# State sums, gate and output turn of a Mamba scan: from channels in rows to tokens in rows

## The chip, the core and the metric

The kernel runs on one core of a Trainium2 chip. The metric is the device time of one execution in microseconds, the median over runs. The five engines of a core (TensorE or PE, VectorE or DVE, ScalarE or ACT, GpSimd or POOL, SyncE or SP) each work through their own queue in order and meet only at semaphores.

## The reference, cut to what matters

One layer of Mamba with a residual and two norms, then a mixture of experts, for x of 8 sequences x 512 tokens x 256 channels. The part that the change touches:

```python
x_ssm, x_gate = split(x @ in_proj_w.T + in_proj_b)
x_conv = silu(conv4(x_ssm) + conv_b)
B, C = split(x_conv @ bc_w.T + bc_b)
dt = softplus(x_conv @ dt_w.T + dt_b)
# for each of 512 steps, 16 states n for each of 256 channels d
h = h * exp(dt[:, None] * A) + dt[:, None] * B[None, :] * x[:, None]
y = sum_n(h * C) + x * D
out = (y * silu(x_gate)) @ out_w.T + out_b + x      # then layer norms
```

After it, a router (8 experts, the 4 best of each token), experts of 512 inner channels with a clipped gate, the weighted sum and a last layer norm.

## The kernel before

Two big stages share one program. Stage 1 does the Mamba layer, the router and the scatter of rows to the experts' queues in DRAM; stage 2 runs the experts over tiles of 512 queued rows; a short last part does the final norm.

**Stage 1.** A sequence is held with channels in the 128 partitions, two halves of 256 channels, and its 512 tokens along the row. Work goes in rounds, one for each sequence, and every engine's program walks the same 16 slots of a round (`for r in rounds(...)`, `for t in range(SLOTS)`), one slot for each of the 16 states. The order inside a slot is written by hand for each engine. Rounds 3 to 6 are a hardware loop. A round works on several sequences at once: sequence s+1 is projected, convolved and prepared (flag `r.a`), s is scanned (`r.b`), s-1 is gated, projected out and normed (`r.c`), s-2 is routed (`r.d`).

In slot t DVE forms the scan's input (`weigh_inputs`, L1032) and scans 128 x 1024 (`scan`, L1041). ACT makes the decays two slots ahead (`decays`, L822), through a ring of four tiles. POOL multiplies the state by C one slot behind (`read_state`, L1175). PE adds the result two slots behind (`sum_states`, L632 to L642): for each half one f32 matmul with the identity as weights, 512 columns, that accumulates into the PSUM bank `p_y[h]`. The first of a sequence is preceded by x times D, a matmul with a diagonal matrix (L638). An f32 matmul shows as two MATMUL instructions in the trace, a transpose as one.

In slot 2 of the next round DVE's `gate` (L1049) multiplies `p_y` by silu of the gate, waits for the sixteenth sum, writes `y` (channels in partitions) and sets `s_y`. Right behind it DVE reads the router's result (`rank_experts`, L1065). In slot 5 DVE's `take_counts` (L1098) waits for PE's `count` (L683 to L687). PE's order from slot 2 on is: `project` 0 and 1, the sum of slot 0 with its x times D, `project_out` 0 and 1 (`y` as weights, so that its result has tokens in partitions), the sum of slot 1, `count`, `convolve`. ACT takes the output in slot 4 (`take_out`, L844), then come the first norm (`variance`, `apply_norm`), POOL's `scale` and DVE's `residual` in slot 9.

Small products of PE go through two PSUM banks, `p_bank`, taken in turn by a list of names (`Round.blocks`); each name waits until the one two places earlier has been read. In slot 8 PE makes `dt0`, `dt1` and `bc`, in slots 10 and 11 the two halves of the gate (`project(r, 2)` and `(r, 3)`), which ACT stores with their bias (`store_in`, L763) and later turns to silu (`silu_gate`).

Of the kernel before, what the change touches and what calls it, by code (L numbers as in the profile page):

```python
# [9 lines left out]
BF16 = mybir.dt.bfloat16  # L10
# [6 lines left out]
P = 128  # L17
# [36 lines left out]
class Round:  # L54
# [13 lines left out]

    def blocks(self):
        d, a, c = self.d, self.a, self.c  # L70
        return (["tr0", "tr1", "rt"] * d + ["in0", "in1"] * a + ["o0", "o1"] * c + ["cnt"] * d + ["cv0", "cv1"] * a
                + ["dt0", "dt1", "bc", "in2", "in3"] * a)

    def block(self, name):
# [90 lines left out]
def build(nc, ctx, ins, out):  # L165
    def sem(name):
        return ctx.enter_context(nc.semaphore(name))

    def sb(name, *shape, dt=F32, at=ctx):
        return at.enter_context(nc.sbuf_tensor(name, [P, *shape], dt))  # L170
# [91 lines left out]
    b_parts = sb("b_parts", D, dt=BF16, at=one)  # L262
    x = sb("x", TT, D, at=one)
    y = sb("y", HALVES, LEN, at=one)
    z = sb("z", TT, D, at=one)
    row_sum = sb("row_sum", 2, TT, at=one)
    var = sb("var", 2, TT, at=one)
# [29 lines left out]
    s_offset, s_t = sem("s_offset"), sem("s_t")  # L297
    s_route, s_rexp, s_chosen, s_index = (sem(n) for n in ("s_route", "s_rexp", "s_chosen", "s_index"))
    s_table = sem("s_table")
    s_scrap = sem("s_scrap")  # L300
    s_left = sem("s_left")
    s_scat = [sem(f"s_scat{i}") for i in range(2)]
# [265 lines left out]
    def pe_stage1(pe):  # L568
        pe.wait_ge(s_first, FIRST_SETUP)

        def order_rate():

            pe.wait_ge(s_const, SETUP)
            for h in range(HALVES):
                mm = pe.transpose(p_y[h][0:STATE, 0:P], raw_rate[:, STATE * h:STATE * (h + 1)], ident[:, :])
            mm.then_inc(s_order, 1)
# [27 lines left out]
        def project(r, m):  # L604
# [3 lines left out]
                pe.wait_ge(s_xt, 16 * (r.s.at(1).n + 1))  # L608
            product(bank[:, :], columns(IN + m * P, P), lambda k: xt[:, k, :]).then_inc(done, 1)

        def convolve(r, h, some):

            if r.like == Round.FIRST:
                pe.wait_ge(s_set_dve, 2)
            if 0 in some:
                bank, _ = block(r, f"cv{h}")
                src, n = r.block(f"in{h}")
                pe.wait_ge(bank_read[src], n)
            b, _ = r.block(f"cv{h}")
            for j in some:  # L620
                mm = pe.matmul(p_bank[b][:, :], taps[:, TAPS * h + j, :], xpad[:, h, j:j + LEN],
                               start=(j == 0), stop=(j == TAPS - 1))
            if TAPS - 1 in some:
                mm.then_inc(bank_full[b], 1)
# [7 lines left out]
        def sum_states(s, t):  # L632

            n = SLOTS * s.n + t
            if t == 0:
                after(pe, s_y, s.n)
                for h in range(HALVES):
                    pe.matmul(p_y[h][:, :], skip_w[:, h, :], xc[s.p][:, h, :], start=True, stop=False)  # L638
            pe.wait_ge(s_read, n + 1)
            for h in range(HALVES):  # L640
                mm = pe.matmul(p_y[h][:, :], ident[:, :], read[:, t % 4, h, :], start=False, stop=(t == SLOTS - 1))  # L641
            mm.then_inc(s_added, 1)  # L642

        def project_out(r, b):

            bank, done = block(r, f"o{b}")
            s = r.s.at(-1)
            if b == 0:
                pe.wait_ge(s_y, s.n + 1)
            for i in range(2):  # L650
                to = bank[:, i * D:(i + 1) * D]
                at = (2 * b + i) * P
                product(to, lambda k: y[:, k, at:at + P], columns(OUT, D), stop=False)
                pe.matmul(to, ones[0:3, :], b_parts[0:3, :], start=False, stop=False)
                if b == 0 and i == 0:
                    pe.wait_ge(s_offset, s.n + 1)
                mm = pe.matmul(to, ident[:, :], x[:, 2 * b + i, :], start=False, stop=True)
            mm.then_inc(done, 1)
# [20 lines left out]
        def count(r):  # L679
# [9 lines left out]
                               skip_group_check=True)  # L689
            mm.then_inc(done, 1)  # L690

        for r in rounds(pe):
            for t in range(SLOTS):
                if t < 2 and r.c:
                    sum_states(r.s.at(-1), SLOTS - 2 + t)
                if r.last and t == 0:
                    transpose_tile(pe, Seq(0, 0))
                    up_projection(pe, Seq(0, 0), 0)
                if r.d and t == 0:
                    transpose_rows(r, 0)  # L700
                    transpose_rows(r, 1)
                if r.d and t == 1:
                    route(r)
                if r.a and t == 2:
                    project(r, 0)
                    project(r, 1)
                if r.c and t == 3:
                    project_out(r, 0)
                    project_out(r, 1)
                if r.last and t == 4:  # L710
                    up_projection(pe, Seq(0, 0), 1)
                if r.d and t == 4:
                    count(r)
                if r.a and t == 4:
                    convolve(r, 0, range(TAPS))
                if r.a and t in (5, 6):
                    half = TAPS // 2 * (t - 5)
                    convolve(r, 1, range(half, half + TAPS // 2))
                if r.like == Round.FIRST and t == 5:
                    order_rate()  # L720
                if r.a and t == 8:
                    for i in range(HALVES):
                        from_xc(r, f"dt{i}", DT_ + i * P, P)
                    from_xc(r, "bc", BC, 2 * STATE)
                if r.like == Round.FIRST and t == 9:
                    place_rate()
                if r.a and t in (10, 11):
                    project(r, t - 8)
                if t >= 2 and r.b:
                    if t == 2 and r.like == 0:  # L730
                        pe.wait_ge(s_set_dve, SET_DVE)
                    sum_states(r.s, t - 2)


    def act_stage1(act):
# [20 lines left out]
        def store_in(r, m):  # L756

            s = r.s.at(1)
            bank, done = full(act, r, f"in{m}")
            if m == 2:  # L760
                after(act, s_y, s.n - 1)
            to = xpad[:, m, TAPS - 1:TAPS - 1 + LEN] if m < 2 else sg[s.p][:, m - 2, :]
            act.activation(to, bank[:, :], ACT.Identity, bias=b_in[:, m:m + 1]).then_inc(done, 1)  # L763

        def store_conv(r, h):
            s = r.s.at(1)
# [65 lines left out]
        def start_total(r):  # L832
# [3 lines left out]
            act.dma_start(total_rows[bass.ds(s.n, 1), :, :, :].rearrange("s p t d -> (s p) t d"),  # L836
                          rows[s.p][:, :, 0:D]).then_inc(s_total[s.p], 16)

        def take_out(r, b):

            bank, done = full(act, r, f"o{b}")
            for i in range(2):
                t = 2 * b + i
                last = act.activation(z[:, t, :], bank[:, i * D:(i + 1) * D], ACT.Copy, accum_out=row_sum[:, 0, t:t + 1])  # L844
            last.then_inc(done, 1)
# [32 lines left out]
        for r in rounds(act):  # L878
            for t in range(SLOTS):

                if r.d and t == 3:
                    router_exp(r)
                if r.a and t == 7:
# [68 lines left out]
    def dve_setup(dve):  # L952

        dve.memset(table[:, :], 0.0).then_inc(s_set_dve, 1)
        dve.wait_ge(s_first, FIRST_SETUP)
        for i in range(HALVES * TAPS):
            dve.tensor_scalar(taps[:, i, :], ident[:, :], tap[:, i // TAPS, i % TAPS:i % TAPS + 1], None, ALU.mult)
        for h in range(2):
            last = dve.memset(xpad[:, h, 0:TAPS - 1], 0.0)
        last.then_inc(s_set_dve, 1)  # L960
        steps = Steps(dve, s_raw, 0, 10)
        steps.then(dve.tensor_tensor(b_bc[:, :], b_bc[:, :], b_or_c[:, :], ALU.mult))
        dve.tensor_reduce(b_bc2[:, :], b_bc[:, :], AX.X, ALU.add).then_inc(s_set_dve, 1)

        dve.wait_ge(s_const, SETUP)
        steps.then(dve.tensor_tensor(b_rest[:, :], b_out[:, :], ln_b[:, :], ALU.subtract))
        steps.then(dve.memset(b_parts[:, :], 0.0))
        for i in range(3):
            steps.then(dve.tensor_copy(b_part[:, :], b_rest[:, :]))
            if i < 2:  # L970
                steps.then(dve.tensor_tensor(b_rest[:, :], b_rest[:, :], b_part[:, :], ALU.subtract))
            steps.then(dve.scalar_tensor_tensor(b_parts[:, :], b_part[:, :], ident[:, i:i + 1], b_parts[:, :],
                                                ALU.mult, ALU.add))

    def dve_setup_rest(dve):
        dve.memset(neg_half[:, :], -0.5)
# [21 lines left out]
    def dve_stage1(dve):  # L998
# [45 lines left out]
        def gate(r):  # L1044
            s = r.s.at(-1)
            dve.wait_ge(s_added, SLOTS * (s.n + 1))
            dve.wait_ge(s_silu, 2 * s.n + 2)
            for h in range(HALVES):
                last = dve.tensor_tensor(y[:, h, :], p_y[h][:, :], sg[s.p][:, h, :], ALU.mult)  # L1049
            last.then_inc(s_y, 1)  # L1050

        def residual(r):
# [634 lines left out]
```

## Time and profile before

| | us |
|---|---|
| median of 3 runs | 1368.25 (1363.77 to 1369.27) |
| profiled execution, its own time | 1371.27 |
| its span, first to last instruction | 1369.4 |
| PE busy, share of the span | 1168.3, 85% |
| DVE busy | 1061.2, 77% |
| ACT busy | 899.0, 66% |
| POOL busy | 792.0, 58% |
| start of the first and of the last `drive` (L1023) | 36.5 and 538.0 |

The page gives the busy time of each engine, the span in 40 slices, the chain that ended last and the costliest groups of instructions. PE counts as busy while a matmul is in its pipeline. The granted clock of TensorE is given for any stretch as a share of full speed: 1.00 is 2.4 GHz, 0.50 is 1.2 GHz; between them a stretch holds both.

### The profile page before, as it was taken

Reading aid. Unit: us, or ns where it says so; the run is one execution under the profiler, and the core shown is the slowest. Engines: PE = TensorE matmul, PEld = TensorE weight load, DVE = VectorE, ACT = ScalarE, POOL = GpSimd, SP = SyncE. Lnnn points to the kernel's source line nnn. Section 1 sums busy time; section 2 is a strip of 40 time slices with the busy share of each in tenths; the row PEclk is TensorE's granted clock in tenths of the full one; section 3 lists DMA queues with packets and bytes.
Section 4 is the critical chain, followed back from the end, with each engine's and each line's share of the span. In section 5 each row is a group of like instructions: output and inputs, shape, how many; then the busy total and the mean of one; then the engine's idle time right before and its main releaser. Section 6 shows DMA issues by size and latency. Waiting matters only on the chain. (4 is left out here: it accounts for less than half of the span.)

```text
span 1369.4 us, 18063 instructions
## 1 busy us (share of the span) xinstructions
PE 1168.3 (85%) x5138; PEld 802.5 (59%) x5138; DVE 1061.2 (77%) x1558; ACT 899.0 (66%) x1551; POOL 792.0 (58%) x566
## 2 busy tenths in 40 slices
PE   7879697988969797765799999999999999999940
PEld 3324252434334343324588888888888888888840
DVE  2999899999989999994777777777777777777744
ACT  4775849485856768425467777767767776767734
POOL 0457568888878888897643444444444444444342
PEclk9899999999999999887899999999999999999985
DMA  2543434545443545336676655566565655565537
GB/s 97 206 155 123 171 107 172 172 149 180 146 167 149 205 150 170 136 104 241 233 216 161 161 144 136 149 158 160 158 160 159 160 139 138 147 163 159 159 38 246
DMA packets 69258, 217.18 MB, mean 159 GB/s; under 512 B 7520, under 2 KB 43232, under 8 KB 56288
## 3 DMA queue, kind: packets, MB, share of 16 engines
q1 hardware_dynamic: 29664, 167.42, 34.0%
q0 software_dynamic: 26880, 36.72, 15.7%
q10 hardware_dynamic: 12672, 12.58, 2.8%
q8 instruction: 14, 0.23, 0.1%
q14 instruction: 28, 0.23, 0.1%
HBM read 165.54 MB, written 51.15 MB: 158 GB/s over the span
## 5 line engine op out<-in xcount | busy, mean ns | idle before, releaser
L641 PE MATMUL p_y<-read,small 128*128 128x512 f32 x512 | 260.4, 644 | 84.2 <-POOL read L1175 84.2
L1041 DVE TENSOR_TENSOR_SCAN state<-decay,p_bu 128x1024 f32<-128x1024 f32 x128 | 292.5, 2285 | 19.3 <-ACT decay L822 10.2
L1497 POOL DMA_INDIRECT total<-o_v,tok x144 | 266.0, 1847 | 45.4 <-issue 45.3
L641 PEld LDWEIGHTS p_y<-read,small 128*128 128x128 f32 x512 | 100.8, 205 | 226.9 <-POOL read L1175 123.3
L1495 POOL TENSOR_TENSOR scrap<-neg_half 128x1 f32<-128x1 f32 x36 | 13.0, 362 | 319.8 <-ACT o_v L1404 317.3
L822 ACT ACTIVATE decay<-dt,scan_rate 128x511 f32<-128x511 f32 x256 | 165.2, 713 | 20.6 <-DVE state L1041 20.2
L1175 POOL TENSOR_TENSOR read<-state,bc 128x1024 f32<-128x1024 f32 x64 | 150.2, 2353 | 34.5 <-DVE p_bu L1032 17.6
L505 ACT ACTIVATE gate_v<-p_g,bias 128x512 f32<-128x512 f32 x144 | 98.5, 684 | 103.0 <-PE p_up L495 96.8
L1217 POOL DMA_INDIRECT queues<-rows,index x128 | 134.4, 1050 | 31.7 <-issue 28.9
L1391 ACT ACTIVATE ah<-a_v 128x512 fp32r<-128x512 f32 x144 | 91.2, 633 | 93.0 <-DVE a_v L519 89.3
L1175 POOL TENSOR_TENSOR read<-state,first_wh 128x1024 f32<-128x1024 f32 x32 | 75.4, 2357 | 65.3 <-DVE p_bu L1032 51.7
L513 DVE TENSOR_SCALAR up_v<-up_v 128x512 f32<-128x512 f32 x144 | 61.5, 427 | 66.6 <-ACT up_v L508 55.7
L1442 DVE TENSOR_TENSOR al<-a_v,ah 128x512 fp32r<-128x512 f32 x144 | 98.8, 686 | 12.4 <-ACT ah L1391 12.4
L519 DVE SCALAR_TENSOR_TENSOR a_v<-gate_v,up_v 128x512 f32<-128x512 f32 x144 | 99.7, 692 | 4.9
L508 ACT ACTIVATE up_v<-p_up,bias 128x512 f32<-128x512 f32 x144 | 98.2, 682 | 0.0
L1175 POOL TENSOR_TENSOR read<-state,first_wl 128x1024 f32<-128x1024 f32 x32 | 75.2, 2352 | 31.2 <-DVE p_bu L1032 21.5
L1364 PE MATMUL p_o<-first_wh,ah 128*128 128x256 f32 x288 | 83.2, 289 | 3.9 <-DVE al L1442 3.9
L1032 DVE TENSOR_TENSOR p_bu<-p_u,bc 128x1024 f32<-128x1024 f32 x64 | 78.9, 1233 | 7.0 <-DVE state L1041 0.5
L1364 PE MATMUL p_o<-wh,ah 128*128 128x256 f32 x288 | 81.9, 284 | 1.6 <-DVE al L1442 1.6
L1364 PE MATMUL p_o<-first_wl,ah 128*128 128x256 f32 x288 | 81.4, 283 | 0.0
L1364 PE MATMUL p_o<-first_wh,al 128*128 128x256 f32 x288 | 81.3, 282 | 0.0
L1364 PE MATMUL p_o<-wh,al 128*128 128x256 f32 x288 | 80.4, 279 | 0.0
(222 smaller groups left out, 3014.7 us busy)
## 6 DMA issues: line engine op xcount, KB each, us to landing
bc<-bc_rows SPq DMA_DIRECT2D x32, 1024.0 KB, 4.9
first_raw<-in_w_experts SPq DMA_DIRECT2D x19, 1668.0 KB
raw_w<-in_w_experts SPq DMA_DIRECT2D x18, 1668.0 KB
first_wh<-bc_rows SPq DMA_DIRECT2D x16, 1024.0 KB
first_wl<-bc_rows SPq DMA_DIRECT2D x16, 1024.0 KB
first_rows<-queues SPq DMA_DIRECT2D x19, 544.0 KB
xq<-queues SPq DMA_DIRECT2D x18, 544.0 KB
queues<-pad SPq DMA_DIRECT2D x9, 544.0 KB
```

The source lines that it names most:

```text
L505: act.activation(gate_v[i % 2][:, :], p_g[i % 2][:, :], ACT.Silu, bias=bias[t.p][:, 0, i:i + 1], scale=ALPHA)
L508: act.activation(up_v[i % 2][:, :], p_up[i % 2][:, :], ACT.Identity, bias=bias[t.p][:, 1, i:i + 1])\
L519: dve.scalar_tensor_tensor(a_v[i % 2][:, :], gate_v[i % 2][:, :], TOP, up_v[i % 2][:, :], ALU.min, ALU.mult)\
L641: mm = pe.matmul(p_y[h][:, :], ident[:, :], read[:, t % 4, h, :], start=False, stop=(t == SLOTS - 1))
L822: act.activation(decay[t % AHEAD][:, h, 1:LEN], dt[s.p][:, h, 1:LEN], ACT.Exp, scale=rate[:, h, t:t + 1])\
L1041: dve.tensor_tensor_scan(flat(state[t % 4][:, :, :]), flat(decay[t % AHEAD][:, :, :]), p_bu[:, :], 0.0, ALU.mult, ALU.add).then_inc(s_stat ...
L1175: pool.tensor_tensor(read[:, t % 4, :, :], state[t % 4][:, :, :], of_state(t, 1), ALU.mult).then_inc(s_read, 1)
L1217: pool.indirect_dma_start(queues, bass.IndirectOffsetOnAxis(ap=index[s.p][:, i:i + 1], axis=0), rows[s.p][:, i // TOPK, :], None).then_inc ...
L1364: mm = pe.matmul(to, v[:, i, a * P:(a + 1) * P], w[t.p][:, c:c + D], start=(i == 0 and a % 2 == 0 and m == 0), stop=(i == CH - 1 and m == ...
L1391: act.activation(ah[:, i, :], a_v[i % 2][:, :], ACT.Copy).then_inc(s_ah, 1)
L1442: dve.tensor_tensor(al[:, i, :], a_v[i % 2][:, :], ah[:, i, :].bitcast(F32), ALU.subtract).then_inc(s_al, 1)
L1497: pool.indirect_dma_start(total, bass.IndirectOffsetOnAxis(ap=tok[t.p][:, a:a + 1], axis=0), o_v[t.p][:, a, :], None, compute_op=ALU.add). ...
```

## The change

Four parts. (1) `sum_states`: the product of state and C is now the weights, and the identity the moving operand, in 128 x 128 blocks with the transpose flag, eight for each slot, accumulating in PSUM; `p_y` then holds tokens in partitions. x times D becomes eight f32 matmuls of 128 columns for two of 512. (2) The gate is projected with tokens in partitions; since its bias then lies along the row, it is added by a bf16 matmul of three rows of `gate_parts`, the bias split in three bf16 parts, which are made at the start. (3) `gate` writes `y_rows`; PE turns it back with eight transposes through two more turns of the small banks (`turn_rows`), ACT copies them to `y` (`take_turned`), and `project_out` waits for both copies. (4) ACT stores the gate with Copy, without a bias.

```diff
-        return (... ["in0", "in1"] * a + ["o0", "o1"] * c + ["cnt"] * d + ...
+        return (... ["in0", "in1"] * a + ["yt0", "yt1", "o0", "o1"] * c + ["cnt"] * d + ...
@@ pe_stage1
+        def spread_gate_bias():
+            for h in range(HALVES):
+                mm = pe.matmul(p_bu[:, h * P:(h + 1) * P], b_in[:, HALVES + h:HALVES + h + 1].broadcast_to([P, P]),
+                               ident[:, :], start=(h == 0), stop=True, skip_group_check=True)
+            mm.then_inc(s_gate_bias, 1)
+        def project_gate(r, b):
+            bank, done = block(r, f"in{HALVES + b}")
+            if r.like == Round.FIRST and b == 0:
+                pe.wait_ge(s_set_dve, 4)
+            for i in range(2):
+                to, at = bank[:, i * D:(i + 1) * D], (2 * b + i) * P
+                product(to, lambda k: xt[:, k, at:at + P], lambda k: w[:, k, IN + D:IN + 2 * D], stop=False)
+                mm = pe.matmul(to, ones[0:3, :], gate_parts[0:3, :], start=False, stop=True)
+            mm.then_inc(done, 1)
@@ sum_states
+            def of_rows(h, b):
+                return p_y[b // 2][:, b % 2 * D + h * P:b % 2 * D + (h + 1) * P]
                 for h in range(HALVES):
-                    pe.matmul(p_y[h][:, :], skip_w[:, h, :], xc[s.p][:, h, :], start=True, stop=False)
+                    for b in range(TT):
+                        pe.matmul(of_rows(h, b), xc[s.p][:, h, b * P:(b + 1) * P], skip_w[:, h, :],
+                                  start=(h == 0 and b % 2 == 0), stop=False, skip_group_check=True)
             for h in range(HALVES):
-                mm = pe.matmul(p_y[h][:, :], ident[:, :], read[:, t % 4, h, :], start=False, stop=(t == SLOTS - 1))
+                for b in range(TT):
+                    mm = pe.matmul(of_rows(h, b), read[:, t % 4, h, b * P:(b + 1) * P], ident[:, :], is_transpose=True,
+                                   start=False, stop=(t == SLOTS - 1), skip_group_check=True)
+        def turn_rows(r, h):
+            bank, done = block(r, f"yt{h}")
+            if h == 0:
+                pe.wait_ge(s_y, r.s.at(-1).n + 1)
+            for b in range(TT):
+                mm = pe.transpose(bank[:, b * P:(b + 1) * P], y_rows[:, b, h * P:(h + 1) * P], ident[:, :])
+            mm.then_inc(done, 1)
@@ project_out
-            if b == 0:
-                pe.wait_ge(s_y, s.n + 1)
+            for h in range(HALVES):
+                src, n = r.block(f"yt{h}")
+                pe.wait_ge(bank_read[src], n)
@@ the loop of PE
+        spread_gate_bias()
                 if r.c and t == 3:
+                    turn_rows(r, 0)
+                    turn_rows(r, 1)
                     project_out(r, 0)
                 if r.a and t in (10, 11):
-                    project(r, t - 8)
+                    project_gate(r, t - 10)
@@ act_stage1, store_in for m of 2 and 3
+                last = act.activation(sg[s.p][:, m - 2, :], bank[:, :], ACT.Copy)
+        def take_turned(r, h):
+            bank, done = full(act, r, f"yt{h}")
+            act.activation(y[:, h, :], bank[:, :], ACT.Copy).then_inc(done, 1)
@@ the loop of ACT, ahead of all else in slot 3
+                if r.c and t == 3:
+                    take_turned(r, 0)
+                    take_turned(r, 1)
@@ dve_setup; in_parts is the loop that made b_parts before
+        dve.wait_ge(s_gate_bias, 1)
+        steps.then(dve.tensor_copy(b_rest[:, :], p_bu[:, 0:D]))
+        in_parts(gate_parts)
@@ gate
-                last = dve.tensor_tensor(y[:, h, :], p_y[h][:, :], sg[s.p][:, h, :], ALU.mult)
+                last = dve.tensor_tensor(flat(y_rows[:, 2 * h:2 * h + 2, :]), p_y[h][:, :], sg[s.p][:, h, :], ALU.mult)
```

## Rows read from the trace of the kernel before

The views cut runs of one kind of instruction together: x8 at the end of a row means eight instructions, and the time is that of all of them.

**Rows 1.** The page's first part, busy us and share of each engine.
```profile
PE 1168.3 (85%) x5138; PEld 802.5 (59%) x5138; DVE 1061.2 (77%) x1558; ACT 899.0 (66%) x1551; POOL 792.0 (58%) x566
```

**Rows 2.** Waits of DVE from 100 to 700 us: total us, times, longest.
```profile
DVE state L1041 <- ACT decay L822: 10.2, 13, 1.5
...
DVE place L1098 <- PE p_bank L687: 5.2, 3, 3.4
```

**Rows 3.** Timeline of PE, one round: start us, us, what, [idle before <-releaser].
```profile
397.94 1.98 PE L641 MATMUL p_y<-read,small 128*128 128x512 f32 x4 [3.08 <-POOL read L1175]
...
404.68 1.98 PE L598 MATMUL p_bank<-first_raw,w 128*128 128x512 f32 x4 [1.26 <-DVE lg L1065]
406.50 1.88 PE L638 MATMUL p_y<-xc,skip_w 128*128 128x512 f32 x4
408.22 1.88 PE L641 MATMUL p_y<-read,small 128*128 128x512 f32 x4
409.94 1.03 PE L598 MATMUL p_bank<-w,y 128*128 128x256 f32 x4
...
418.49 0.24 PE L687 MATMUL p_bank<-chosen,ones 128*128 128x32 bf16 x4
```

**Rows 4.** Timeline of DVE in the same round.
```profile
404.45 0.18 DVE L1065 TENSOR_TENSOR lg<-p_bank,small 128x32 f32<-128x32 f32 x1
...
417.59 1.23 DVE L1032 TENSOR_TENSOR p_bu<-p_u,bc 128x1024 f32<-128x1024 f32 x1
418.77 0.19 DVE L1098 TENSOR_TENSOR place<-p_bank,base 128x32 f32<-128x32 f32 x1
```

**Rows 5.** Timeline of PE, next round: eight transposes and what follows.
```profile
470.94 1.04 PE L665 MATMUL p_bank<-small,rows 128*128 128x128 f32 x8
471.81 1.88 PE L641 MATMUL p_y<-read,small 128*128 128x512 f32 x4
```

**Rows 6.** Timeline of PE, last rounds: transposes, then matmuls on their copies.
```profile
646.56 1.07 PE L665 MATMUL p_bank<-small,rows 128*128 128x128 f32 x8
648.46 1.92 PE L675 MATMUL p_bank<-small,x1t 128*128 128x8 f32 x16 [0.83 <-ACT x1t L871]
```

**Rows 7.** Timeline of PE where the clock was low.
```profile
462.00 5.13 PE L641 MATMUL p_y<-read,small 128*128 128x512 f32 x8 [5.46 <-POOL read L1175]
...
551.34 3.78 PE L638 MATMUL p_y<-xc,skip_w 128*128 128x512 f32 x4 [2.40 <-DVE y L1049]
554.91 2.96 PE L641 MATMUL p_y<-read,small 128*128 128x512 f32 x4
```

**Rows 8.** Stretches: busy us (x) of PE, PEld, DVE, ACT, POOL; PEclk; DMA.
```profile
393.00:396.00 3.00, 1.85 (x11) 1.09 (x9) 1.73 (x2) 1.47 (x3) 0.46 (x1) 1.00 0.01 4
...
462.00:465.00 3.00, 3.00 (x4) 1.44 (x5) 2.86 (x3) 2.99 (x5) 2.83 (x2) 0.51 0.97 288
```

**Rows 9.** Timeline of PE, then of ACT, at the dt projection of that round.
```profile
433.64 3.70 PE L598 MATMUL p_bank<-xc,w 128*128 128x512 f32 x8 [1.06 <-ACT xc L776]
...
438.50 0.68 ACT L790 ACTIVATE first_raw<-p_bank,small 128x512 f32<-128x512 f32 x1
...
440.68 0.68 ACT L813 ACTIVATE bc_out<-p_bank,b_bc 32x512 f32<-32x512 f32 x1 [0.93 <-PE p_bank L598]
```

**Rows 10.** Timeline of PE, then of DVE, at the start.
```profile
6.05 6.12 PE L598 MATMUL p_bank<-first_raw,w 128*128 128x512 f32 x8 [6.05 <-DMA small<-in_small]
...
9.52 0.43 DVE L966 TENSOR_TENSOR b_rest<-set_up,small 128x256 f32<-128x256 f32 x1 [1.56 <-DMA set_up<-in_set_up]
...
13.19 0.48 DVE L972 SCALAR_TENSOR_TENSOR b_parts<-b_part,small,b_parts 128x256 bf16<-128x256 bf16 x1
...
31.63 1.23 DVE L1005 SCALAR_TENSOR_TENSOR rest<-rest,expo 128x1024 f32<-128x1024 f32 x1 [14.72 <-ACT rest L801]
```

**Rows 11.** Timeline of PE, then of DVE, after the last scan.
```profile
620.04 1.10 PE L598 MATMUL p_bank<-w,y 128*128 128x256 f32 x4 [1.22 <-DVE y L1049]
...
627.24 0.19 DVE L1098 TENSOR_TENSOR place<-p_bank,base 128x32 f32<-128x32 f32 x1 [3.42 <-PE p_bank L687]
```

More of the change, by code:

```diff
@@ L70, in blocks @@
         d, a, c = self.d, self.a, self.c
-        return (["tr0", "tr1", "rt"] * d + ["in0", "in1"] * a + ["o0", "o1"] * c + ["cnt"] * d + ["cv0", "cv1"] * a
+        return (["tr0", "tr1", "rt"] * d + ["in0", "in1"] * a + ["yt0", "yt1", "o0", "o1"] * c + ["cnt"] * d + ["cv0", "cv1"] * a
                 + ["dt0", "dt1", "bc", "in2", "in3"] * a)
@@ L264, in build @@
     y = sb("y", HALVES, LEN, at=one)
+    y_rows = sb("y_rows", TT, D, at=one)
+    gate_parts = sb("gate_parts", D, dt=BF16, at=one)
     z = sb("z", TT, D, at=one)
@@ L299, in build @@
     s_table = sem("s_table")
+    s_gate_bias, s_y_rows = sem("s_gate_bias"), sem("s_y_rows")
     s_scrap = sem("s_scrap")
@@ L761, in store_in @@
                 after(act, s_y, s.n - 1)
-            to = xpad[:, m, TAPS - 1:TAPS - 1 + LEN] if m < 2 else sg[s.p][:, m - 2, :]
-            act.activation(to, bank[:, :], ACT.Identity, bias=b_in[:, m:m + 1]).then_inc(done, 1)
+            if m < 2:
+                last = act.activation(xpad[:, m, TAPS - 1:TAPS - 1 + LEN], bank[:, :], ACT.Identity, bias=b_in[:, m:m + 1])
+            else:
+                last = act.activation(sg[s.p][:, m - 2, :], bank[:, :], ACT.Copy)
+            last.then_inc(done, 1)
         def store_conv(r, h):
@@ L963, in dve_setup, with in_parts @@
         dve.tensor_reduce(b_bc2[:, :], b_bc[:, :], AX.X, ALU.add).then_inc(s_set_dve, 1)
+        def in_parts(to):
+            steps.then(dve.memset(to[:, :], 0.0))
+            for i in range(3):
+                steps.then(dve.tensor_copy(b_part[:, :], b_rest[:, :]))
+                if i < 2:
+                    steps.then(dve.tensor_tensor(b_rest[:, :], b_rest[:, :], b_part[:, :], ALU.subtract))
+                steps.then(dve.scalar_tensor_tensor(to[:, :], b_part[:, :], ident[:, i:i + 1], to[:, :], ALU.mult, ALU.add))
+        dve.wait_ge(s_gate_bias, 1)
+        steps.then(dve.tensor_copy(b_rest[:, :], p_bu[:, 0:D]))
+        in_parts(gate_parts)
         dve.wait_ge(s_const, SETUP)
         steps.then(dve.tensor_tensor(b_rest[:, :], b_out[:, :], ln_b[:, :], ALU.subtract))
[L967 to L973, printed above, removed]
+        in_parts(b_parts)
     def dve_setup_rest(dve):
```

## The prediction

> **What bounds the kernel now.** I read the page's first part, then the waits of DVE in stage 1, then one steady round (about 391 to 465 us) as timelines of PE and DVE, and last the places where TensorE's clock was low. PE is the busiest engine over the whole span [rows 1], but that average mixes a stage 2 that PE fills with a stage 1 that it doesn't. While the scans run, DVE waits for others very little: 10.2 us in 13 pieces for a decay of ACT, 5.2 us in three for PE's count [rows 2]. PE in the same rounds waits for POOL, up to 5.46 us at a time [rows 7]. So stage 1 is DVE's, and a cheaper sum on PE is worth nothing by itself. It counts only where DVE waits for PE, directly or through ACT.
>
> There are two such places, and the reader should see how tight the first is. After the router's result (L1065 at 404.45) PE goes without a pause through `project` 1, x times D, sum 0, `project_out`, sum 1 and `count` [rows 3]. Its last matmul starts at 418.49, and DVE takes the counts 0.28 us later, at 418.77 [rows 4]. DVE's instruction before it runs from 417.59 to 418.82. So the two chains, 14 us long, end together, and whatever is added to PE's there stops DVE and all that follows. The second is slot 8: ACT reads `dt1` at 438.50 and waits 0.93 us for `bc` [rows 9], and the pieces of 1.5 us for a decay [rows 2] are the end of that ACT chain.
>
> **The change part by part.** All sums are for the profiled execution (1371.27 us, span 1369.4), 3.0 us above the median of the runs; the differences are then put on the median.
>
> *The sums.* One sum was 1.72 us (408.22 to 409.94, [rows 3]). Eight transposes of this size take 0.87 us from start to start (470.94 to 471.81, [rows 5]). Accumulating ones aren't in the trace; I take the same, and 1.72 us as the upper end, since they could go as the f32 matmuls do. The saving is 0.85 us for each of 128 sums, 109 us of PE time, nearly all in time that PE would wait anyway. On the path to the count lie sums 0 and 1: 1.70 us less. x times D streams the same columns (1.72 us, 406.50 to 408.22, [rows 3]) in 16 instructions for 4; at the 0.11 us of a transpose each that is 1.75 us. I cost it at nothing; 0.3 us more is the other end.
>
> *The turn.* After it come eight transposes, two ACT copies of 128 x 512 and only then `project_out`. The same pattern stands in the last round: transposes from 646.56, first matmul on their copies at 648.46, so 1.90 us [rows 6]. On ACT the copies stand first in slot 3. Queued behind them are the router's exponent, which DVE wants in slot 6, and the decays of slot 5, wanted by the scan right behind 418.77 us [rows 4]; with ACT held until about 411 us both are in time. The count is therefore 1.90 - 1.70 = 0.2 us later with the clock at full speed. From both sides: 0.7 us earlier if the copies overlap PE better, 1.9 us later if the sums save nothing. I take 0.2, since both of its terms are whole rows of this shape.
>
> *The clock.* This is the largest term. Now PE does a sum of four f32 matmul instructions of 512 columns in each slot (on average 4.5 us: 36.5 to 538.0 over 7 rounds of 16), and the clock holds 1.00 through most of it, but falls after longer pauses: after 5.46 us of waiting eight matmuls took 5.13 us for 3.44 + 0.16 = 3.60 [rows 7], at a granted clock of 0.51 [rows 8]; after 2.40 us, with only tiny matmuls before it, two groups of four ran from 551.34 to 557.87, 6.53 us for 3.60. One cold start thus costs 1.5 to 2.9 us; I take 2.2. With half the work in each sum the pauses become longer and the work between them thinner, so I expect the clock at 1.2 GHz through slots 12 to 15 and at the start of the next round, and again ahead of slot 8.
>
> At the start of a round PE has a pause of 1.26 us before `project` 1 [rows 3] that takes up 1.3 of the 2.2, and some of the slow work is sum 15, for which nobody waits. I keep 0.6 us. With the turn's 0.2 this is 0.8 us in each of the five rounds that both project and count: **4.0 us**. Bounds: -0.7 x 5 = -3.5, and (2.9 - 1.3 + 1.9) x 5 = 17.
>
> Ahead of slot 8 PE paused 1.06 us before `dt0` [rows 9]. With three sums less of 0.85 us behind the convolution, and one of them still tied to POOL, that pause grows to about 4 us, and `dt0`, `dt1` and `bc` (12 matmuls) start cold. `dt1` would be done near 437.3 and is read at 438.50: 1.2 us of cover. The rest, 1.0 us, moves `bc`, the softplus and the decay on which DVE already waits; I take 0.8 in the six rounds that show that wait: **4.8 us**. Bounds: 0 if the clock holds, (2.9 - 1.2) x 6 = 10.
>
> *The last round* has no scan to hide anything. DVE's early plan holds the gate back, so shorter sums win nothing; `project_out` starts at 620.04, and DVE then waits 3.42 us for the count [rows 11]. The norm, the first expert rows and the first weights all hang on this. The turn adds 1.9; a cold start adds 2.2, less a little where the clock happens to be up: **3.9 us**. Bounds: 1.0 and 1.9 + 0.9 (transposes at half speed) + 2.9 = 5.7. Round 7, which no longer projects, starts cold already [rows 7]; two sums less against one turn is +0.2 there, counted as nothing.
>
> *The start.* `spread_gate_bias` puts four instructions of 128 columns before the first projection, whose eight of 512 took 6.12 us [rows 10]: a quarter of 0.77 each, four times, is 0.77; at full clock 0.43. I take **0.6 us**, all on the path. DVE's ten added small instructions: the same chain for the output bias ran from 9.52 to 13.67, 4.2 us, and lies ahead of 14.72 us of waiting [rows 10]; nothing, unless that wait went.
>
> *The gate projected by rows.* Per round 16 instructions of 256 columns for 8 of 512, and four small bf16 ones. Four of 256 took 1.03 us [rows 3], so four groups with their bias are 4.2 to 5.3 us for 3.44. Three to four sums before it are shorter, and after it PE waits for POOL up to 5.46 us [rows 7]; nothing, and at the first sequence at most 1 us. DVE's `gate` keeps its shape, ACT's Copy for Identity likewise. No DMA is added, and SP's and POOL's queues keep their order; the next sequence's x still waits for the last gate block, many slots ahead.
>
> The sum: 0.6 + 4.0 + 4.8 + 3.9 = 13.3 us. On the median: 1368.25 + 13.3 = **1381.5 us**.
>
> **A rule against the trace.** From 393 to 396 us, with one sum's end and eight transposes in it, the clock was 1.00 [rows 8]; after a pause of 3.08 us the next four matmuls took the 1.98 us of full speed [rows 3]. The Trainium skill (TensorE: Matmul & The Clock Gate, Part 4: PE-mode transpose) says that transposes don't raise the clock as matmuls do. By it every stretch with sums alone would be cold without exception, and the time that of rival 2; this stretch speaks against it, but it held real matmuls as well and doesn't settle it.
>
> **The rivals.**
> 1. *The clock holds.* Then 0.6 + 5 x 0.2 + 1.9 = 3.5 us: 1371.8. For it: the stretch at 393 us. Against it: the same PE fell to half speed at 551 us after 2.40 us of pause [rows 7], and the change makes such pauses the rule.
> 2. *Transposes do not count for the clock at all.* Every cold start is full length: (2.9 - 1.3 + 0.2) x 5 = 9.0, (2.9 - 1.2) x 6 = 10.2, 5.7 at the end, 0.8 at the start: 25.7 us, 1394.
> 3. *Accumulating transposes cost as much as the matmuls they replace.* Then the clock stays as before, and the turn is paid whole: 1.9 x 5 + 1.9 + 0.6 = 12.0 us, 1380. Nothing in the trace is like it; it is only not excluded.
> 4. *Not slower: the path to the count gets shorter.* If from the first transpose to `project_out` passes less than the 1.70 us that sums 0 and 1 give back, the count comes before DVE asks. At 1.2 us for the turn the waits for the count in rounds with scans, 5.2 - 3.42 = 1.8 us [rows 2, 11], go; with +0.6 at the start and +1.2 at the end the time is 1368. For it: ACT is idle then. Against: the 1.90 us row is this very pattern.
>
> **How the numbers follow.** Forecast 0.44, rival 1 0.22, rival 2 0.11, rival 3 0.09, rival 4 0.08, and 0.06 for something unseen, faster. A change of 0.5% (6.8 us) is what a measurement of this kernel can tell. The forecast's own range is 1374 to 1390, a few hundredths of it inside 0.5%; rivals 2 and 3 are slower, 1 and 4 the same. Slower 0.62, same 0.31, faster 0.07. The range that leaves out 2 in 10 runs from 1368 to 1394.
>
> **What would show it.** Right: `sum_states` at 0.87 to 1.7 us for eight; a granted clock of 0.50 at 1.2 GHz in the last slots of most rounds and at L598 of `dt0`; DVE idle at L1098 (place) near 1 us in each steady round, waiting for PE; more than 10.2 us of waiting for decays; `y_rows` transposes to `project_out` in about 1.9 us; and the first expert matmuls (L495) some 13 us later, with stage 2 unchanged behind it. Wrong: no wait at L1098 and a mean clock as high in stage 1 as before would make it rival 1 or 4; a sum of 1.7 us at clock 1.00, rival 3; a stage 2 of another length would be something that I haven't seen.

## The result and the profile after

The changed kernel takes **1381.07 us** (median of 4 runs, 1380.30 to 1381.91) against 1367.73 us of the kernel before on the same chip (4 runs): ratio 1.0107, 95% interval 1.0091 to 1.0123. Four more runs on another chip gave 1382.28 against 1366.70, ratio 1.0108 (1.0091 to 1.0124). The change makes the kernel slower by about 1%, as forecast. The profiled execution took 1381.58 us, with a span of 1379.7 against 1369.4.

The page's first part and its clock row answer to [rows 1]: 36 us less of PE, and a clock that falls in stage 1 (0.88 over the span, 0.95 before).

```profile
PE 1132.4 (82%) x5910; PEld 891.7 (65%) x5910; DVE 1067.1 (77%) x1568; ACT 906.7 (66%) x1567; POOL 791.5 (57%) x566
...
PEclk9778797887958797756799999999999999999985
```

DVE's waits from 100 to 700 us answer to [rows 2] (total us, times, longest):

```profile
DVE place L1157 <- PE p_bank L726: 13.5, 8, 8.5
...
DVE state L1100 <- ACT decay L867: 9.0, 8, 1.5
...
DVE first_raw L1067 <- ACT x1t L849: 6.8, 6, 1.1
...
DVE p_bu L1091 <- issue: 5.7, 1, 5.7
```

The wait for PE's count went from 5.2 to 13.5 us. The wait for decays went from 10.2 to 9.0 us, though the prediction named more than 10.2 as a sign of being right; the lost time shows in front of it, in a wait of the same chain, `first_raw` for ACT's x1t, 1.1 us in each of six rounds (1.7 us in all before). The last row was 3.3 us before, and is nobody's work: DVE without instructions at the loop's edge.

One round of PE (the one after the loop's edge), as [rows 3]: start, us, what, [idle before <-releaser].

```profile
407.06 1.97 PE L669 MATMUL p_y<-small,read 128*128 128x128 f32 x8 [4.70 <-POOL read L1234]
408.82 3.42 PE L714 MATMUL p_bank<-small,x1t 128*128 128x8 f32 x16
412.09 5.10 PE L608 MATMUL p_bank<-first_raw,w 128*128 128x512 f32 x8
417.02 1.95 PE L664 MATMUL p_y<-skip_w,xc 128*128 128x128 f32 x16
418.81 1.04 PE L669 MATMUL p_y<-small,read 128*128 128x128 f32 x8
419.68 1.04 PE L679 MATMUL p_bank<-small,y_rows 128*128 128x128 f32 x8
421.46 1.13 PE L608 MATMUL p_bank<-w,y 128*128 128x256 f32 x4 [0.74 <-ACT y L887]
...
429.27 0.24 PE L726 MATMUL p_bank<-chosen,ones 128*128 128x32 bf16 x4
...
444.48 7.81 PE L608 MATMUL p_bank<-xc,w 128*128 128x512 f32 x12 [4.38 <-ACT xc L821]
```

Eight accumulating transposes take 0.87 us from start to start (418.81 to 419.68), as plain ones do. From the turn's first transpose to `project_out` it is 1.78 us. `project` 0 and 1 took 5.10 us where 3.60 is full speed, and the dt products 7.81 us behind a pause of 4.38.

**Where the 10.3 us of span are.** The interval of two scans is the difference of their starts in DVE's timeline. First scan: 39.05 to 40.19, +1.1. Last scan: 606.22 to 618.45, so 11.1 us between the two: the intervals of scans 4 to 5, with the count, +3.1; those of scans 9 to 11, with the decay, in six rounds, +5.8; scan 8 to 9 of round 1, behind a late residual, +0.7; the loop's edge +2.4; all others -0.9. From the last scan to the first expert matmul +5.1. That makes 17.3 us at the first expert matmul (641.52 to 658.79). Then 7.4 us come back between the 1st and the 49th of them, and the rest of stage 2 is 0.5 longer.

### The profile page after: what moved, and what is told of

It is laid out like the page before. It is cut to its first block and busy times, and to the rows that moved or that the text cites. A ratio compares the mean times of both kernels' runs of the same rounds, so it can differ in the third digit from the quotient of the medians.

```text
span 1379.7 us, 19658 instructions
## 1 busy us (share of the span) xinstructions
PE 1132.4 (82%) x5910; PEld 891.7 (65%) x5910; DVE 1067.1 (77%) x1568; ACT 906.7 (66%) x1567; POOL 791.5 (57%) x566
## 5 line engine op out<-in xcount | busy, mean ns | idle before, releaser
L669 PE MATMUL p_y<-small,read 128*128 128x128 f32 x1024 | 174.8, 330 | 125.3 <-POOL read L1234 125.2
L669 PEld LDWEIGHTS p_y<-small,read 128*128 128x128 f32 x1024 | 146.2, 171 | 162.3 <-POOL read L1234 145.4
L867 ACT ACTIVATE decay<-dt,scan_rate 128x511 f32<-128x511 f32 x256 | 164.4, 711 | 19.8 <-DVE state L1100 17.3
L608 PE MATMUL p_bank<-xc,w 128*128 128x512 f32 (+1 forms) x96 | 60.0, 783 | 26.4 <-ACT xc L821 26.4
```

Of the source, the lines that this page charges most:

```text
L669: mm = pe.matmul(of_rows(h, b), read[:, t % 4, h, b * P:(b + 1) * P], ident[:, :], is_transpose=True, start=False, stop=(t == SLOTS - 1), ...
L867: act.activation(decay[t % AHEAD][:, h, 1:LEN], dt[s.p][:, h, 1:LEN], ACT.Exp, scale=rate[:, h, t:t + 1])\
```

## The experiments

Each kernel's waits, clock and intervals are read from its own trace. e1 to e4, e5 to e8 and e9 to e12 each shared a chip and its runs of the kernel before (1375.10, 1366.70 and 1373.30 us, the last a single run).

**Fill.** PE's lost work is put back as a product with zeros:

```diff
@@ sum_states, changed kernel
+            if t >= 2:
+                pe.matmul(p_y[0][:, :], zeros[:, :], read[:, t % 4, 0, :], start=False, stop=False, ...)
```

> The changed kernel with one more matmul in each sum of slots 2 to 15: 512 f32 columns of the product against a tile of zeros, added to p_y. It adds nothing to the result and brings PE's work per sum back to what it was (about 1.72 us). Theory (the low clock costs the time): the clock stays at 1.00 ahead of slot 8 and at the start of most rounds; the intervals with the decay wait (slot 10 to 11, together 5.8 us longer than before) fall back to those of before, the counts cost 0.2 to 0.3 us a round, and the time comes to about 1372 (1370 to 1375). Rival (the turn, with its two copies, costs the time, not the clock): more work on PE gives nothing back, 1381 or more.

1384.27 us, ratio 1.0065 (1.0046 to 1.0085); clock 0.943. The intervals of scans 9 to 11 fell from 75.1 to 69.6 us in sum (69.3 before); those of scans 4 to 5 from 29.0 to 27.4 (25.9 before). More work on PE makes the kernel shorter (ratio 1.0065 for 1.0107), so the clock is a real part of the loss, and nearly the whole of the decay part. The time missed what was expected: it is 9 us above the kernel before, where 4 were forecast. What the fill leaves is as in the changed kernel: the edge (9.38), 1.3 us in the round behind it, and 40.1 us from the last scan to the first expert matmul (40.3; 35.3 before).

**The three parts alone.** The next three kernels are cut out of the change, so that values stand in other places of `y` or of the gate than the reference has them. The router then chooses otherwise, and the experts get 912 of the first-layer matmuls instead of 864, one step of stage 2 or about 36 us more. Their totals are not comparable; their stage 1 is.

```diff
@@ e2: the kernel before, with yt0 and yt1 in the list, turn_rows, take_turned
@@ e3: the changed kernel without those
@@ e4: the kernel before with spread_gate_bias, gate_parts and project_gate
```

> The kernel before with the turn alone: the gated values go through y_rows, eight transposes, two ACT copies and then project_out; sums and gate as before (so its output holds values in the wrong places). Theory: the clock is as before, the turn is paid whole at the count, 1.9 us in each of five rounds, less what was idle, and 2 to 3 us after the last scan; the decay intervals don't change. 1377 to 1380. Rival (turn costs little, since PE waits anyway): within 2 us of before, 1368 to 1370.

> The changed kernel without the turn: gate writes y directly, project_out waits for s_y alone (its output is wrong, since y is not turned). Theory: the clock is low at the same places; the decay intervals stay 5 to 6 us longer than before in all, while the wait for the count goes or shrinks below that of before, and the start stays 1.1 us later: 1372 to 1376. Rival (the shorter sums are harmless, all of the cost is the turn): 1367 to 1369.

> The kernel before with the gate projected by rows and its bias in parts, no turn and the old sums (its output is wrong, since the gate is laid out the other way). Theory: the first scan starts about 1.1 us later, because the first decays stand behind the last gate store on ACT; nothing else: 1368.5 to 1370. Rival (the longer gate blocks hold up slots 10 and 11 of every round): 0.5 us or more in each of seven rounds, 1372.

From the first to the last scan (567.2 us before, 578.3 after), turn alone 580.5, sums and gate without the turn 569.4, gate alone 567.9. With the turn alone the intervals of scans 4 to 5 in rounds 4 and 6 are 6.01 for 4.07, so a turn costs 1.94 on that path; in the changed kernel, with its shorter sums, they are 4.39, so 0.32. Without the turn they are 4.01, but the intervals of 9 to 11 are 73.7 in sum: the sums alone let the clock fall (0.885). The gate alone costs nothing in the decay intervals (69.2 in sum), 2.1 at the loop's edge (9.09 for 7.03), and 1.0 from scan 4 to 5 in the round behind it. So the theory of e2 held; that of e3 held in kind (the sum of scans 9 to 11 grew by 4.4, not by 5 to 6); that of e4 had nothing of the edge.

**Fill with transposes**, for rival 2:

```diff
@@ e1 with, for its zero matmul
+                for h in range(HALVES):
+                    for b in range(TT):
+                        pe.matmul(of_rows(h, b), zeros[:, :], ident[:, :], is_transpose=True, start=False, ...)
```

> The changed kernel with eight more accumulating transposes (weights all zero, so nothing is added) in the sum of slots 2 to 15. With the zero matmul of 512 columns in that place the mean clock went from 0.88 to 0.94, the interval between scans 9 and 11 from about 8.6 back to 7.5 us. The eight transposes keep PE busy as long as that matmul (0.87 us at full clock). My theory (what counts is how long PE works): clock near 0.94, the decay interval back at 7.5 us, the count interval near 4.4. Rival 2 of the prediction (transposes do not count at all): clock stays at 0.87 or lower, slots 12 to 15 at 1.2 GHz, decay interval 8.5 us or more, and the time longer than the changed kernel's by 5 to 15 us, since eight transposes more at half speed are 1.7 us in each slot.

1376.51 us, ratio 1.0064 (1.0046 to 1.0081); clock 0.944; 69.6 us for scans 9 to 11 (the 8.6 and 7.5 us above are scans 10 to 11 of one round alone). It does just what the matmuls did. In PE's timeline of this kernel, where a round begins after a pause at 1.2 GHz, nothing but transposes runs, and their time falls to that of full speed:

```profile
315.83 1.97 PE L671 MATMUL p_y<-small,zeros 128*128 128x128 f32 x8 [5.46 <-POOL read L1241]
317.59 1.91 PE L675 MATMUL p_y<-small,read 128*128 128x128 f32 x8
319.29 1.51 PE L671 MATMUL p_y<-small,zeros 128*128 128x128 f32 x8
320.64 1.04 PE L675 MATMUL p_y<-small,read 128*128 128x128 f32 x8
```

The stretches view (busy us (x) of PE, PEld, DVE, ACT, POOL; PEclk; DMA) has the clock at 0.50 and then at 1.00:

```profile
316.00:320.00 4.00, 4.00 (x20) 4.00 (x21) 3.86 (x4) 3.99 (x7) 3.53 (x3) 0.50 0.99 307
320.50:322.50 2.00, 1.18 (x11) 0.94 (x9) 1.90 (x2) 0.04 (x1) 1.97 (x2) 1.00 0.97 326
```

In the changed kernel the same place, with one set of transposes in each slot and pauses between, stays at 1.2 GHz:

```profile
316.54 1.97 PE L669 MATMUL p_y<-small,read 128*128 128x128 f32 x8 [5.49 <-POOL read L1234]
318.84 1.97 PE L669 MATMUL p_y<-small,read 128*128 128x128 f32 x8 [0.33 <-POOL read L1234]
323.65 1.97 PE L669 MATMUL p_y<-small,read 128*128 128x128 f32 x8 [2.84 <-POOL read L1234]
```

So it is how much PE works, not the kind of instruction. The rule that the prediction took from the Trainium skill (TensorE: Matmul & The Clock Gate, Part 4: PE-mode transpose), whose transposes are bf16, does not hold here, for f32 transposes.

**The count one slot later**, in the changed kernel (e6) and in the one before (e7):

```diff
-                if r.d and t == 5:
+                if r.d and t == 6:
                     take_counts(r, route_steps)
```

> The changed kernel with take_counts (and the copy of base that follows it) moved from DVE's slot 5 to slot 6, so that DVE asks for PE's count one scan later. Theory: the wait for the count in rounds 2 to 7 is a real loss; it goes (it was 0.6 to 2.3 us a round above a slot of 3.8) and nothing else of the round is late: 3 to 5 us less than the changed kernel. Rival: PE's convolution, the decays or the residual in slot 9 are late by the same chain, and what slot 5 gives comes back there: less than 1 us. The wait of about 8.5 us in the last round, where there is no scan, stays in both.

> The kernel before with take_counts one slot later. Its waits for the count with a scan running were 1.8 us in all. Theory: 1 to 2.5 us faster than the kernel before, and the only version so far that beats both. Rival: the count's readers (POOL's scatter, the ring of small banks) are moved along and take it back: within 0.5 us.

> The changed kernel itself, as the comparison for the others on the same chip: 1.009 to 1.012 of the kernel before. Its profile is a second sample: the fetch of instructions at the loop's edge (9.46 us from scan 15 of round 4 to scan 0 of round 5, against 7.03 before) comes out near 9.4 again if it belongs to the program, and elsewhere between 7 and 9.5 if it is chance; the wait of 6.4 us of the last place for a fetch, gone in the first profile of this kernel, stays gone or comes back by the same reasoning.

e6: 1381.71 us, ratio 1.0106 (1.0090 to 1.0123), beside 1.0108 of the changed kernel. e7: 1366.57, ratio 1.0005 (0.9990 to 1.0019). **My theory fell** in both. e8, the changed kernel again, has an edge of 9.25 us and 578.2 us from first to last scan (9.46 and 578.3 in its first trace), so both belong to the program; the wait of 6.4 us stays gone. DVE's waits of e6:

```profile
DVE place L1157 <- PE p_bank L726: 9.0, 2, 8.6
DVE state L1100 <- ACT decay L867: 8.8, 7, 1.5
DVE state L1100 <- DVE p_bu L1091: 7.9, 39, 0.2
DVE first_raw L1067 <- ACT x1t L849: 6.8, 6, 1.1
```

The wait for the count is gone from all rounds with scans; it was about 4.5 us (13.5 less 9.0), and the time from first to last scan went from 578.3 to 577.9. The intervals of scans 4 to 5 lost 6.4 us (29.0 to 22.6), those of 5 to 6, with the moved work, gained 2.9, those of 9 to 11 gained 3.2 (75.1 to 78.3). Count and decay are two places at which DVE meets one chain: `project`, turn, `project_out`, norm, convolution, dt, softplus, decay. Whoever waits less at the first waits longer at the second. This is shown for the changed kernel, round by round: in round 5 the two intervals around the count lose 1.25 us net and the decay's gains 1.33, in round 4 it is 0.21 and 0.34.

The kernel before shows something else. In e7 the decay intervals don't grow (69.2 for 69.3), and the time from first to last scan is 1.6 us less (565.6 for 567.2). But 1.4 of that is round 7, where the one trace of the kernel before has a wait that e4, e11 and e12 haven't (scans 4 to 5 take 5.34 us there, 4.20 in these). In rounds 3 to 6 there was hardly a wait to move.

**Fill in parts.** e9 has the fill in slots 2 to 5 alone, e10 in 12 to 15 alone (`if 2 <= t <= 5`, `if t >= 12`).

> The changed kernel with the zero matmul of 512 columns only in the sums of slots 2 to 5, just ahead of the dt projection. Theory, as it stands after the late count gave nothing: projection, turn, project_out, norm, convolution, dt, softplus and decay are one chain, on which DVE waits in two places; cold time taken out at either place shortens the round by itself. Here: the granted clock ahead of dt0 back at 1.00, the interval from scan 9 to 11 back by about 1 us in each round (from 12.3 to 11.3), the count intervals as in the changed kernel (4.4 to 6.1 us), rounds of 74.4 to 74.6 us. Rival (the clock at dt depends on the whole round, not on what stands just ahead): the decay intervals stay at 12.3.

> The same with the zero matmul only in slots 12 to 15. Theory: the clock is up when the next round's projection and turn come, the count intervals come near 4.4 in all rounds (5.0 and 6.1 before), the decay intervals stay near 12.3, and the round is 0.3 to 0.6 us shorter than the changed kernel's 75.0 to 75.6. Rival: with the count earlier the dt projection starts earlier too but PE is as cold there, so that the decay interval grows by what the count gives.

e9, one run, 1383.27 us: scans 9 to 11 at 69.6 us in sum, 5.5 less than in the changed kernel, as the theory has it. From first to last scan it is 574.6 us (578.3), only 3.7 less: 0.9 went back in the count interval of round 5, behind the edge (7.02 for 6.09), and 0.7 in scans 11 to 12. PE's timeline at dt in round 4, where the changed kernel paused 4.35 us and took 8.05 for 12:

```profile
359.11 3.70 PE L609 MATMUL p_bank<-xc,w 128*128 128x512 f32 x8 [0.91 <-ACT xc L824]
364.12 1.90 PE L609 MATMUL p_bank<-xc,w 128*32 128x512 f32 x4 [1.31 <-ACT expo L839]
```

e10, one run, 1389.45 us: scans 4 to 5 at 27.5 (29.0), 9 to 11 at 74.4 (75.1), 577.2 from first to last scan. So the fall of the clock ahead of dt is 4 to 5 of the 11 us, and that at the start of a round 1 to 2. Neither total says much beside one run of before at 1373.30; e10 has 3 us more in stage 2, as e7 has, for which I have no cause.

**The loop's edge.** e11 is the kernel before with DVE's ten small instructions at the start made twice; e12 projects each half of the gate in four pieces:

```diff
@@ e11, dve_setup
+        for _ in range(2):
             steps.then(dve.tensor_tensor(b_rest[:, :], b_out[:, :], ln_b[:, :], ALU.subtract)) ...
@@ e12, project, for m of 2 and 3
+                for i in range(4):
+                    mm = product(bank[:, i * P:(i + 1) * P], columns(IN + m * P, P), lambda k: xt[:, k, i * P:(i + 1) * P])
```

> The kernel before with DVE's chain for the bias parts made twice at the start (the ten small instructions more that the change adds there; the second time gives the same values). It tells where the 2.1 to 2.4 us at the loop's edge come from (scan 15 of round 4 to scan 0 of round 5: 7.0 us in the kernel before and with the turn alone, 9.1 to 9.5 in every kernel with the gate by rows). If it is DVE's own code, moved in memory by the longer start: 9.1 to 9.5. If it is PE's longer loop body, or the sum of the engines' fetches: 7.0.

> The kernel before with each half of the gate projected in four pieces of 128 columns instead of one of 512 (the same values, as many PE instructions more in the loop's body as the gate by rows has and a few over). If PE's longer body makes the loop's edge longer: 9 us or more. If DVE's moved code does: 7.0. Nothing else should move: PE has slack where the gate stands.

e11 (one run, 1379.53 us): the edge takes 9.01 us, and DVE's timeline shows the hole:

```profile
390.54 2.27 DVE L1042 TENSOR_TENSOR_SCAN state<-decay,p_bu 128x1024 f32<-128x1024 f32 x1
398.09 1.23 DVE L1033 TENSOR_TENSOR p_bu<-p_u,first_wh 128x1024 f32<-128x1024 f32 x1 [5.28 <-issue]
```

e12 (one run, 1377.14): the edge 7.13. So it is DVE's ten instructions at the start, and not PE's longer loop. All the traces agree: the ten with these instructions have edges of 9.01 to 9.57 us, the four without 6.93 to 7.13. How ten instructions that ran long before can do it is argued, not shown: they move DVE's code in memory. The Trainium skill (Runtime: NRT & Kernel Launch, Instruction fetch mechanics) says that a taken branch out of the pages that are loaded stops an engine until its code has come by DMA. The traces show code coming at each edge, but how much comes doesn't go with the edge's length: between 390 and 405 us the instruction queue q14 moved 7 packets of 8 KB in the changed kernel and 3 in the kernel before, but also 7 in e2, whose edge is 7.0, and 3 in e11, whose edge is 9.0.

The hole goes on. POOL and PE stand behind it, PE's clock falls, and the projection of the next round runs at 1.2 GHz:

```profile
401.98 3.78 PE L641 MATMUL p_y<-read,small 128*128 128x512 f32 x4 [5.07 <-POOL read L1176]
405.55 3.42 PE L675 MATMUL p_bank<-small,x1t 128*128 128x8 f32 x16
408.83 6.38 PE L598 MATMUL p_bank<-first_raw,w 128*128 128x512 f32 x8
```

In e11 scan 4 to 5 of that round took 8.02 us where the rounds on both sides took 4.08: a kernel with not one instruction more in any round lost 6.4 us from first to last scan (573.6 for 567.2), 2.0 at the edge and 4.0 behind it; 1.3 more, in round 3, stand ahead of the edge and have no cause here.

But the edge alone doesn't decide what the round behind it loses. In e12 it took 7.56 with an edge like before's; its pause at that place was 3.19 us and the clock fell, where 3.08 us of pause in [rows 3] left it up:

```profile
400.84 3.04 PE L646 MATMUL p_y<-read,small 128*128 128x512 f32 x4 [3.19 <-POOL read L1180]
403.67 3.42 PE L680 MATMUL p_bank<-small,x1t 128*128 128x8 f32 x16
```

And e5, with the fill, took 4.32 behind an edge of 9.39.

## Why the prediction was right, and where it was not

The time was forecast to 0.5 us (1381.5; measured 1381.07), and that closeness is luck: the mechanism was right, but the terms of the two traces sum to 17.8 us where 13.3 were forecast, and a wait that is not the change's took some of that off again. Of the rivals, 1 is out by the clock, 2 by e5, 3 by the sums and 4 by the turn. One by one:

- **The start, 0.6.** It was 1.1, and not where I put it. `spread_gate_bias` took 1.22 us, but the projection behind it came up to full speed sooner (4.56 us for the 6.12 of [rows 10]), and `drive` stands 0.5 us earlier than before. That is one trace's luck: in e8, the same kernel, the projection took 6.17 us and the first scan stands at 44.06 for 40.19. What belongs to the change is DVE's wait for the first decays, 1.7 us in both traces and none before. The first gate block is late, that I had allowed "at most 1 us". PE makes it mostly at 1.2 GHz, and ACT has its store ahead of the first decays:

```profile
34.83 0.58 ACT L807 ACTIVATE sg<-p_bank 128x512 f32<-128x512 f32 x1
37.85 0.60 ACT L807 ACTIVATE sg<-p_bank 128x512 f32<-128x512 f32 x1 [2.45 <-PE p_bank L629]
38.34 3.76 ACT L867 ACTIVATE decay<-dt,scan_rate 128x511 f32<-128x511 f32 x6
```

- **The sums, 0.85 us less each.** Right: 0.87 us at full speed. At half speed they take 1.7, as forecast for slots 12 to 15. Rival 3 is out.
- **The turn, 0.2 on the path to the count.** Measured 0.32 in the rounds where the clock is up (4.39 for 4.07). With 1.78 us to `project_out` it takes more than the 1.70 that the sums give back, so rival 4 is out.
- **The clock at the start of a round, 0.6 in five rounds.** With the turn, 4.0 was forecast for the five count intervals; they grew by 3.96, in pieces of 0.32, 0.97, 0.32, 2.03 and 0.32. Three of the five rounds lose nothing to the clock, and the 2.03 stand in the round after the loop's edge, which is no part of this step. Round 7 gave 0.9 back, that I had counted as nothing; it belongs to the interval of 5.34 us that is 4.20 in e4, e11 and e12, and is no gain of the change. The sum was right, its pieces were not.
- **The clock ahead of slot 8, 4.8.** Right in mechanism, a little short in size: 5.8, and 0.7 in round 1. The pause was forecast at about 4 us and was 4.38; `dt1` is read 0.9 to 1.2 us late, and `bc` 0.65 behind that. e9, which takes away the cold start alone, has 5.5 us of it back (3.7 net).
- **Two places, two terms.** This was the wrong picture. I added the count's term to the decay's because DVE waited at both. e6 shows one chain: the sum holds, but the count's wait is no loss of its own. e7 doesn't show that for the kernel before; it shows that of the 1.8 us that rival 4 hoped to win there more than 1 was a wait of that one trace.
- **The last round, 3.9.** It was 5.1 between these two traces, and 3.2 to 5 by all of them. PE's timeline, as [rows 11]:

```profile
632.25 0.63 PE L679 MATMUL p_bank<-small,y_rows 128*128 128x128 f32 x4 [0.43 <-DVE y_rows L1108]
633.13 0.89 PE L679 MATMUL p_bank<-small,y_rows 128*128 128x128 f32 x4 [0.25 <-DVE lg L1124]
634.80 2.04 PE L608 MATMUL p_bank<-w,y 128*128 128x256 f32 x4 [0.78 <-ACT y L887]
...
638.11 1.91 PE L608 MATMUL p_bank<-w,y 128*128 128x256 f32 x4
...
640.81 1.03 PE L608 MATMUL p_bank<-w,y 128*128 128x256 f32 x4
```

  The turn took 2.55 us (632.25 to 634.80) for 1.90: its second half waits until DVE has read the router's result out of the same small bank, a turn of the ring that I had not followed. `project_out` up to the count took 9.5 us for 6.9. The fills don't help here (13.4 and 13.5 us from DVE's gate to the place, 13.7 without, 14.0 with the turn and full sums). The clock falls in `project_out` in all eight traces with the turn. The turn's own short pauses are near at hand as the cause, but it falls there in four of the six traces without a turn as well (e3, e4, e7, e12). In [rows 11] four instructions take 1.10 us; this is e4:

```profile
623.56 1.10 PE L608 MATMUL p_bank<-w,y 128*128 128x256 f32 x4 [1.22 <-DVE y L1085]
...
625.74 1.91 PE L608 MATMUL p_bank<-w,y 128*128 128x256 f32 x4
```

  From the last scan to the first expert matmul these four take 36.8 to 36.9 us, the kernel before and e11 35.3, and the eight with the turn 40.1 to 40.6. So the turn costs 3.2 to 3.8 us here against the four and about 5 against the two.
- **Not in the prediction: the loop's edge.** 2.4 us there, and probably most of the 2.03 in the round behind it. I had priced DVE's ten small instructions at the start by the wait that hides them, and so at nothing. Their time is hidden; that they make DVE's program longer isn't.
- **Not in the prediction: 7.4 us back in stage 2**, and not the change's. DVE's last place in the two kernels, before and after:

```profile
661.53 0.19 DVE L1098 TENSOR_TENSOR place<-p_bank,base 128x32 f32<-128x32 f32 x1 [6.40 <-remote]
```

```profile
672.96 0.19 DVE L1157 TENSOR_TENSOR place<-p_bank,base 128x32 f32<-128x32 f32 x1 [0.35 <-PE p_bank L726]
```

  From the 1st to the 49th expert matmul the traces take either 54.3 to 55.2 us (before, and all eight of e1 to e4 and e9 to e12) or 47.5 to 48.3 (the first trace of the changed kernel, and all four of e5 to e8, one of them the kernel before but for a slot). Some 6 of the 7.4 us stand ahead of that last place. They go with the chip or the execution, not with the kernel.

The terms of the two traces sum to 17.8 us without that wait; the medians lie 13.3 and 15.6 apart. If some executions of before carry the 7.4 us and those of after do not, both fit, and the spread of its runs on either chip (1363.8 to 1371.3, 1363.9 to 1370.4) looks like it, but times alone don't show it: how much the change costs where neither has that wait stays open, between 13 and 18 us. The 15.6 are the better guide: all four traces of that chip are without the wait.

No version beat the kernel before; e7 is its equal, and the best form of the change, with fill, is still 0.6% behind.

## What to carry to other kernels

Where two waits of one engine lie along one chain, a delay upstream shows at both, and moving the first wait frees nothing: follow the chain to where it closes before adding terms. Take a second trace of the kernel before, too: 1.1 us in round 7 that three like traces lack, and a clock that held in the last round where four of six traces lost it, both went into the account of the change. An engine with slack can be made faster and the kernel slower, if its work was what kept the clock up for the short products that others wait for. Count added instructions as code too: ten at the start made a loop's edge 2 us longer, and the round behind it lost from 0.3 us (e5) to 4 (e11).

## What the runs showed of the hardware

- f32 transposes of 128 x 128 that accumulate in PSUM start every 0.109 us at 2.4 GHz and every 0.21 to 0.22 at 1.2 GHz, and bring the clock up as matmuls of the same length do (e5 beside e1: 0.944 and 0.943).
- Two pauses of nearly one length went different ways: the clock was up after 3.08 us in the kernel before and down after 3.19 in e12, with nearly the same work ahead. What decides it is not shown.
- A hardware loop's edge costs DVE 3.2 to 3.4 us without instructions in the four traces without the ten instructions at the start, and 5.3 to 5.8 in the ten with them.
- A wait of 5.1 to 6.5 us on "remote", at the first count after the loads of stage 2 begin, comes with some chips or executions and not with others, for whatever kernel.
